# A decoder block's cross-attention: the output product of each head as two fp32r products instead of one fp32 product

## What is computed

```python
q, k, v = (heads(q), heads(k), heads(v))            # 16 heads of 64; 2,113 keys
scale = 1.0 / np.sqrt(np.sqrt(DIM_HEAD))
logits = jnp.einsum('bhqd,bhkd->bhqk', q * scale, k * scale)
w = jax.nn.softmax(logits.astype(jnp.float32), axis=-1).astype(logits.dtype)
out = jnp.einsum('bhqk,bhkd->bhqd', w, v)
out = out.transpose(0, 2, 1, 3).reshape(b, l, INNER)
return out @ Wout                                   # 1,024 -> 256
...
x = _layernorm(x + _L0_xattn_ref(ctx_1024, x, ...), axis=-1)
```

## Time and profile before

| | |
|---|---|
| time, median of 3 runs | 3040.41 us (3039.42 to 3043.43) |
| the profiled execution | 3045.14 us, span of the core 3043.4 us |
| TensorE busy over the span | 2881.4 us, 95% |
| VectorE, ScalarE, GpSimd | 2025.4, 1638.5, 1560.1 us |
| mean granted TensorE clock | 0.981 of full speed |

### The profile page before, as it was taken

One profiled execution on the slowest core, in us unless ns is written; L12 is line 12 of the kernel. 1 busy time (PEld: TensorE's weight loads), 2 busy tenths in 40 slices (PEclk: granted clock), 3 DMA queues, 4 the chain that ended last, 5 costly groups with the idle time before them and its releaser, 6 DMA issues. The chain is left out here.

```text
span 3043.4 us, 36342 instructions
## 1 busy us (share of the span) xinstructions
PE 2881.4 (95%) x12032; PEld 1906.0 (63%) x12032; DVE 2025.4 (67%) x3451; ACT 1638.5 (54%) x2837; POOL 1560.1 (51%) x1235
## 2 busy tenths in 40 slices
PE   7577999999999999999999999999999999899997
PEld 3234565656665656565656565656777777687786
DVE  5897777775658677666687767566555555356666
ACT  5753545453545454535454545366777777525652
POOL 4495757670017575600175756003656667526764
PEclk9898999999999999999999999999999999799999
DMA  6453212111122121211221212110101100421112
GB/s 237 149 180 106 76 36 60 35 53 57 39 70 60 36 66 29 73 37 39 70 67 36 60 36 66 37 39 15 46 20 34 45 17 15 146 74 60 49 46 82
DMA packets 71694, 189.98 MB, mean 62 GB/s; under 512 B 8420, under 2 KB 39272, under 8 KB 63448
## 3 DMA queue, kind: packets, MB, share of 16 engines
q1 hardware_dynamic: 67096, 172.08, 18.7%
q0 software_dynamic: 3984, 15.60, 1.6%
q10 hardware_dynamic: 432, 0.01, 0.0%
HBM read 124.59 MB, written 28.44 MB: 50 GB/s over the span
## 5 line engine op out<-in xcount | busy, mean ns | idle before, releaser
L1148 ACT ACTIVATE a_carry<-a_st 128x512 f32<-128x512 f32 (+1 forms) x1088 | 649.4, 597 | 918.5 <-PE a_st L1590 905.5
L1610 PE MATMUL a_o<-a_carry,a_vals 128*65 128x512 f32 (+1 forms) x1632 | 835.6, 593 | 0.0
L1338 DVE TENSOR_REDUCE a_maxes<-a_mx 128x1 f32<-128x512 f32 x1016 | 677.5, 686 | 189.0 <-PE a_mx L1513 180.9
L964 POOL TENSOR_TENSOR a_plow<-a_carry,a_phigh 128x512 fp32r<-128x512 f32 (+1 forms) x272 | 349.0, 1290 | 259.8 <-ACT a_phigh L1151 256.2
L996 POOL TENSOR_TENSOR a_shared<-a_shared,a_bc 128x512 f32<-128x512 f32 x192 | 250.9, 1307 | 386.7 <-DVE a_shared L1268 386.7
L1590 PE MATMUL a_st<-a_q,a_kone 65*128 65x512 f32 (+1 forms) x1088 | 431.6, 397 | 0.0
L1268 DVE TENSOR_TENSOR_SCAN a_shared<-a_shared 128x512 f32<-128x512 f32 x192 | 290.3, 1514 | 15.9 <-POOL a_shared L983 14.6
L1589 PE MATMUL a_st<-a_q,a_keven 128*128 128x512 f32 (+1 forms) x544 | 295.9, 544 | 2.5 <-ACT a_carry L1148 1.6
L1589 PE MATMUL a_st<-a_q,a_kodd 128*128 128x512 f32 (+1 forms) x544 | 286.8, 527 | 0.0
L1513 PE MATMUL a_mx<-a_kodd,a_q 128*128 128x512 f32 x512 | 275.6, 554 | 10.3 <-DVE a_maxes L1338 9.0
L1590 PEld LDWEIGHTS a_st<-a_q,a_kone 65*128 65x128 f32 (+1 forms) x1088 | 202.0, 186 | 123.6 <-issue 93.2
(11 more groups left out here) (300 smaller groups left out, 5225.3 us busy)
## 6 DMA issues: line engine op xcount, KB each, us to landing
a_bc<-m_kept_bc SPq DMA_DIRECT2D x48, 512.0 KB, 3.7
a_wt<-a_w_split SPq DMA_DIRECT2D x15, 1536.0 KB, 8.6
a_kone<-a_keven SPq DMA_DIRECT2D x32, 528.5 KB, 4.5
a_kone<-a_kodd SPq DMA_DIRECT2D x32, 528.5 KB, 4.2
e_wall<-in_w_t_dram SPq DMA_DIRECT2D x27, 512.0 KB, 5.6
a_shared<-m_kept_bc SPq DMA_DIRECT2D x16, 512.0 KB, 3.9
a_w_split<-a_wt POOLq DMA_DIRECT2D x4, 1536.0 KB, 5.4
a_shared<-in_ctx_dram SPq DMA_DIRECT2D x4, 1536.0 KB
```

Source lines behind the costliest of these rows:

```text
L964: nc.gpsimd.tensor_tensor(p_low(s)[0:r], p_of(s % 4)[0:r], p_high(s)[0:r].bitcast(F32), ALU.subtract).then_inc(p_low_ready, 1)
L1148: nc.scalar.activation(p_of(s % 4)[0:r], st[0:r, s % 2], ACT.Exp, scale=SCALE).then_inc(exp_done, 1)
L1338: nc.vector.reduce_max(maxes[:, c, t:t + 1], mx_bank(g, i), AX_X).then_inc(mx_max, 1)
L1610: nc.tensor.matmul(ps_o[0:DH + 1, g % 2], vals[0:r, kt * HG + j, :], p_of(s % 4)[0:r], start=(kt == 0), stop=(kt == KT - 1)).then_inc(pv_d ...
```

## The change

The one fp32 product of 65 rows becomes two fp32r products into the same bank. The first multiplies high parts: the tile `a_oone` has the output's high part in rows 0 to 63, the sum's high part in row 64 and its low part in row 96 (SUM_LOW), with zeros between, so it takes 97 rows, and 258 columns, an even number. The second has 128 rows: `a_otwo` is the output's low part over its high part, `a_wotwo` the weights' high part over their low part. To make these, ScalarE copies `a_o` twice where it copied once, VectorE has a new piece "o" at tile 4 (`out_low`, two subtractions), and in every fourth head, at tile 12, a new piece "w" splits the loaded weights of four heads (`out_weights_high`, two copies on ScalarE, `out_weights_low`, one subtraction on VectorE). Weights are loaded into one raw buffer after the split of the group before; GpSimd clears other tiles before head 0.

```diff
     b, h = divmod(g, H)
+    if g > 0:
+        at[LAG + 1].append(("o", g - 1, 0))
+    if g % HG == 0:
+        at[12].append(("w", g // HG, 0))
...
             def load_wo(n):
-                sp.dma_start(wo_sb[0:DH, n % 2, :, 0:DM], wo_src[:, n % NG * HG:(n % NG + 1) * HG]).then_inc(wo_loaded, 16)
+                if n > 0:
+                    sp.wait_ge(wo_low, n)
+                sp.dma_start(wo_raw[0:DH], wo_src[:, n % NG * HG:(n % NG + 1) * HG]).then_inc(wo_loaded, 16)
...
-                nc.scalar.activation(o_sb[0:DH + 1, g % 2], ps_o[0:DH + 1, g % 2], ACT.Copy).then_inc(o_out, 1)
+                if g < 2:
+                    act.wait_ge(ones_set, 2)
+                nc.scalar.activation(o_one[0:DH + 1, g % 2], ps_o[0:DH + 1, g % 2], ACT.Copy)
+                nc.scalar.activation(o_two[DH:P, g % 2], ps_o[0:DH, g % 2], ACT.Copy).then_inc(o_out, 1)
+
+            def out_weights_high(n):
+                act.wait_ge(wo_loaded, 16 * (n + 1))
+                act.wait_ge(ones_set, 2)
+                if n > 0:
+                    act.wait_ge(ring_full, AT["O", HG * n - 1, TT - 1] + 1)
+                nc.scalar.activation(wo_one[0:DH, :, 0:DM], wo_raw[0:DH], ACT.Copy)
+                nc.scalar.activation(wo_two[0:DH], wo_raw[0:DH], ACT.Copy).then_inc(wo_high, 1)
...
+            def out_low(g):
+                dve.wait_ge(o_out, g + 1)
+                nc.vector.tensor_tensor(o_two[0:DH, g % 2], ps_o[0:DH, g % 2], o_one[0:DH, g % 2].bitcast(F32), ALU.subtract)
+                nc.vector.tensor_tensor(o_one[SUM_LOW:SUM_LOW + 1, g % 2], ps_o[DH:DH + 1, g % 2],
+                                        o_one[DH:DH + 1, g % 2].bitcast(F32), ALU.subtract).then_inc(o_low, 1)
+
+            def out_weights_low(n):
+                dve.wait_ge(wo_high, n + 1)
+                nc.vector.tensor_tensor(wo_two[DH:P], wo_raw[0:DH], wo_one[0:DH, :, 0:DM].bitcast(F32),
+                                        ALU.subtract).then_inc(wo_low, 1)
...
                     pe.wait_ge(o_out, g + 1)
+                    pe.wait_ge(o_low, g + 1)
                     if g % HG == 0:
-                        pe.wait_ge(wo_loaded, 16 * (g // HG + 1))
+                        pe.wait_ge(wo_low, g // HG + 1)
                 wait_bank(what)
-                nc.tensor.matmul(ring[:, bank(what), 0:DM + 1], o_sb[0:DH + 1, g % 2, t * P:(t + 1) * P],
-                                 wo_sb[0:DH + 1, g // HG % 2, g % HG], start=True, stop=True).then_inc(ring_full, 1)
+                nc.tensor.matmul(ring[:, bank(what), 0:DM + 2], o_one[0:SUM_LOW + 1, g % 2, t * P:(t + 1) * P],
+                                 wo_one[0:SUM_LOW + 1, g % HG], start=True, stop=False)
+                nc.tensor.matmul(ring[:, bank(what), 0:DM], o_two[:, g % 2, t * P:(t + 1) * P],
+                                 wo_two[:, g % HG], start=False, stop=True).then_inc(ring_full, 1)
```

More of the change, by code:

```diff
@@ L472 @@
 LAG = 3
+SUM_LOW = 96
 FD = 3
@@ L603 @@
 BEFORE, BEFORE_ACT, BEFORE_DVE = first("PE"), first("ACT"), first("DVE")
-AFTER = [("O", NH - 1, t) for t in range(TT)] + [("E", B - 1, 0), ("F", B - 1, 0)]
+AFTER = [("o", NH - 1, 0)] + [("O", NH - 1, t) for t in range(TT)] + [("E", B - 1, 0), ("F", B - 1, 0)]
 MADE = BEFORE + [x for g in range(NH) for kt in range(KT) for x in BESIDE[g][kt]] + AFTER
@@ L696, in attention @@
         vals = sb("a_vals", [P, KT * HG, DH + 1])
-        o_sb = sb("a_osb", [P, 2, S])
-        wo_sb = sb("a_wo", [P, 2, HG, DM + 1])
+        o_one = sb("a_oone", [P, 2, S], F32R)
+        o_two = sb("a_otwo", [P, 2, S], F32R)
+        wo_raw = sb("a_woraw", [P, HG, DM])
+        wo_one = sb("a_woone", [P, HG, DM + 2], F32R)
+        wo_two = sb("a_wotwo", [P, HG, DM], F32R)
         lat = shared[:, CTX_T * DM:CTX_T * DM + TT * DM].rearrange("p (t d) -> p t d", d=DM)
@@ L707, in attention @@
         w_out_first = early[:, (FX + FS) * S:(FX + FS + 2) * S].rearrange("p (c d) -> p c d", d=DM)
-        bc_first = [halves[:, 0], halves[:, 1], bc_early, o_sb[:]]
+        bc_first = [halves[:, 0], halves[:, 1], bc_early, o_two[:].bitcast(F32)]
         decay_first, dtu_bank = [mx[:, 0], mx[:, 1], ring[:, 1]], [ps_o[:, 0], ps_o[:, 1]]
@@ L740, in attention @@
         o_out = sem("a_o_out")
+        o_low = sem("a_o_low")
+        wo_high = sem("a_wo_high")
+        wo_low = sem("a_wo_low")
         mx_full = sem("a_mx_full")
@@ L906, in load_weights @@
                 sp.dma_start(wt[:].rearrange("p i k n -> p (i k n)").bitcast(F32), w_dram[n % NG]).then_inc(w_loaded, 16)
-                if n > 1:
-                    sp.wait_ge(ring_full, AT["O", HG * (n - 1) - 1, TT - 1] + 1)
                 load_wo(n)
@@ L943, in set_ones @@
                 s.then_inc(ones_set, 1)
-                nc.gpsimd.memset(wo_sb[DH:DH + 1], 0.0)
-                nc.gpsimd.memset(wo_sb[0:DH, :, :, DM:DM + 1], 0.0).then_inc(wo_cleared, 1)
+                one = wo_one[:].bitcast(F32)
+                nc.gpsimd.memset(o_one[DH:P].bitcast(F32), 0.0)
+                nc.gpsimd.memset(one[DH:P], 0.0)
+                nc.gpsimd.memset(one[0:DH, :, DM:DM + 2], 0.0).then_inc(wo_cleared, 1)
                 pool.wait_ge(wo_cleared, 1)
-                nc.gpsimd.memset(wo_sb[DH:DH + 1, :, :, DM:DM + 1], 1.0).then_inc(ones_set, 1)
+                nc.gpsimd.memset(one[DH:DH + 1, :, DM:DM + 1], 1.0)
+                nc.gpsimd.memset(one[SUM_LOW:SUM_LOW + 1, :, DM:DM + 1], 1.0).then_inc(ones_set, 1)
             def make_rstd(what):
@@ L1139, in make @@
                     decays(*what[1:])
+                elif what[0] == "w":
+                    out_weights_high(what[1])
             def exp(s):
@@ L1380, in make @@
                     row_max(what[1], what[2])
+                elif kind == "o":
+                    out_low(what[1])
+                elif kind == "w":
+                    out_weights_low(what[1])
                 elif kind == "O":
@@ L1597, in add_o @@
                     pe.wait_ge(o_out, g - 1)
+                    pe.wait_ge(o_low, g - 1)
                 if j == 0:
```

## The result

The change makes the kernel slower: 3147.74 us (median of 4 runs, 3144.38 to 3148.97) against 3041.92 us in runs of the kernel before on the same chip, a ratio of 1.035 with a 95% interval of 1.033 to 1.036. The forecast was 3076 us, 36 us more; it became 106. The sign held, the size did not, and the time lies outside the range.

A forecast was written before the change was run, and what follows sets the result against it. TensorE was taken to bound the kernel, waiting on VectorE's row maxima. Terms: -50 + 29 + 12 + 9 + 10 + 19 + 5 + 2 = +36 us, giving 3076 us; range 3012 to 3100, the forecast's own 3050 to 3100.

The forecast's parts named there:

- Products: TensorE's output products, tiles 6 to 9: each 0.43 us becomes 0.24, 256 of them save 50 us.
- the 5: Tiles 6 to 9: 0.4 us of the saving lost in 12 heads where VectorE lacks idle time, 5 us.
- No subtraction of one row is in the trace ... I take 0.69: VectorE's second subtraction in `out_low`, one row of 512: taken as 0.69 us, like 64 rows; 1.4 us together.
- The mechanism, results held up behind `out_low`: Tiles 3 to 5: `out_low`'s 1.4 us on VectorE delays the row maxima that TensorE waits for in tile 5.
- the four terms: Delays by head: odd 29 us, even 9 in batches 0 to 2; odd 12, even 10 in the last batch.
- Without a scan ahead of them it fits. 0.4 on average: Even heads, batches 0 to 2: maxima 0.7 us late in head 22, none without a scan; 9 us in all.
- ScalarE gets a second copy ... I take 0.5: ScalarE in tile 3: the second copy of a head's output, `o_two`, puts off what follows by 0.5 us.
- Weights: Every fourth head, tile 12: ten heads at 1.0 us, two with `norm_var` 1.4, four of last batch 1.5; 19 us.
- The rival on the faster side: Late maxima are made up within the head, so only part of the 86 us costs stays: 2990 to 3033; chance 0.2.
- Worse than forecast: Weights' split holds ScalarE back in last batch, or one-row subtractions wait for each other: 3100 or more; chance 0.08.
- outside the loop: At the end of attention, 0.5 + 1.4 us stand uncovered ahead of the last products: 2 us.

The follow-up runs named there:

- e14: The changed kernel without ScalarE's second copy of a head's output after the first two heads (old values used): 3105.69 us, ratio 1.021 to the kernel before.
- e13: The changed kernel's two products and all their preparation, each piece moved to where VectorE had idle time in the trace of before: 3014.41 us, ratio 0.9915.
- e3: The changed kernel with all fp32r products, but high and low parts made only for the first two heads and first weights, then reused: 3008.22 us, ratio 0.988.
- e6_three: The changed kernel with three fp32r products (65, 65, 64 rows) instead of two, one output copy and one subtraction, same places: 3146.09 us, ratio 1.033.

## Why the prediction was right or wrong

- **Products: the price right, what is kept of it not.** 0.12 us start to start each. The forecast was -50, with 5 not given back. Alone they gave 37 us, so 13 us were not given back: tiles 6 to 9 gain 0.68 us a head for 0.78, and 6.5 us come back in tiles 10 to 14. The row that the 5 rest on is one head's.
- **"No subtraction of one row is in the trace ... I take 0.69": right**, 690 ns. The Trainium skill, "VectorE: DVE Perf Modes", section on the TRN2 errata, gives 0.691 us for 512 elements, with no term for the rows; this trace agrees.
- **The mechanism, results held up behind `out_low`: right.** Tiles 4 and 5 lose 98 us where the four terms made 60. The wrong sizes, by the tile times: odd heads of batches 0 to 2, 39 for 29; even heads there, 27 for 9 (1.6 of it in head 0, which has no `out_low`); odd heads of the last batch 16 for 12, even ones 16 for 10.
- **The step that failed most: "Without a scan ahead of them it fits. 0.4 on average".** It didn't fit in any even head: 0.8 us is the least, 1.1 the mean in batches 0 to 2. The margin was in the trace of before and was read in one head alone, head 22, whose 0.7 us late were taken for the bad case. In every one of the 23 even heads of batches 0 to 2 the first maximum behind the insertion ended only 0.44 to 0.70 us ahead of the product that needs it (0.66 in most, head 22 among them), and 1.4 us were put in front of it: 1.4 less 0.66, with the 0.06 between a maximum's end and its product, is the 0.8 measured. In heads 10, 26 and 42, where a scan also stands behind `out_low`, it is 2.1 to 2.5 us.
- **"ScalarE gets a second copy ... I take 0.5": too small.** 0.48 was the step from the one copy to the decay. Now the second copy starts 0.60 after the first, and what follows starts 0.61 after it. It costs 0.73, and 42 us together with what hangs on it (e14). Why the second copy is left no earlier is not shown. It isn't that both read `a_o`: the step behind it is 0.61 whatever comes next, and the weights' two copies, which also share a source, are 0.95 apart at a length of 1.05. It is the only one of these copies that writes other rows (64 to 127) than it reads (0 to 63).
- **Weights: 19 forecast, 28.8 at tiles 15 and 16.** Head 24 came out as worked out, 1.8, and the ten ordinary heads lost 10.4 together for 10. The heads that also have `norm_var`, forecast 1.4, lost 4.2 and 3.7, and the first head of the last batch, which has it too, 5.6: in VectorE's queue the statistics stand behind the weights' subtraction and ahead of the maxima, so they are put off as well. Each of the three also has a stretch at half clock there.
- **The clock: a term that was missing.** After some waits of 1.0 to 3.2 us TensorE falls to 1.2 GHz for a while. This is at most 27 us of the 106, and some 18 by the heads compared above. The Trainium skill, "TensorE: Matmul & The Clock Gate", Part 1, says that TensorE slows down when it has idled, and its account of the oscillation warns of stalls that bring the slow clock back; the trace agrees in that, though the page doesn't tell which of these short waits does it. It was to be weighed in the forecast of a change that adds stalls.
- **The rival on the faster side: wrong for this placement**, since the maxima were not made up within a head. It is what e13 reaches by other placing. *Worse than forecast*, 0.08, is what happened, though by another mechanism than the one named there.

Together, by the tile sums: 98 for 60 at tiles 4 and 5 (38 us), 29 for 19 at the weights (10), -29 for -45 in all other tiles, the products' (16), 4 for 2 outside the loop (2), and 4 more between the profiled spans (101.8 apart) and the medians (105.8): 70 of 70 us. The last 4 have no cause here; they are what one execution differs from a median. The half-clock stretches are inside the other terms, most plainly in tiles 6 to 9, which gain 43.0 us without them (e3) and 33.7 with. Their 18 us are an estimate from five stretches; no two kernels differ in the stretches alone.

## What to carry to other kernels

Work that is "hidden" on an engine two thirds busy costs its full length if it stands in front of a result that an in-order queue is waiting for: find a place by the idle time per tile, and put it behind the urgent results of that tile, before asking whether the new arithmetic is cheaper. Before work is inserted, read the margin between the first result behind it and whoever waits for that result, in every kind of head and not in one; and read all results behind it, here the K tile's low part as well as the maxima. Stalls have a second price where the slow clock follows them.

## What the runs showed of the hardware

- **64 rows after 65.** A product of 64 rows among products of 65 to 128 costs 0.28 us more than one of 65 rows (0.64 us for three, then 0.36), 74 to 78 us over the kernel. Columns behave otherwise: in the last batch of e6_three value products of 65, 64 and 65 columns start at 2282.09, 2282.33 and 2282.56. The Trainium skill, "TensorEngine Tiling (Array Packing)", Key Properties, says that a change of tiling mode drains TensorE, and lists 64 rows as a mode of its own; the rows agree with it. It lists 64 columns beside 128 rows as a mode too, and there these rows show no such cost.
- **VectorE beside GpSimd.** The weights' subtraction, two operands in SBUF, takes 1.22 us at tile 12 of the change in 13 of 16 heads and 1.36 in three, and a median of 2.12 in e13_by_room, where in most heads GpSimd is already multiplying when it starts. In the three heads with 1.36 it starts 0.24 us ahead of GpSimd's multiplication, and that takes 2.27 us where most take 1.27: both are stretched, the later one more. The Trainium skill, "SBUF — State Buffer", Who interferes with whom, states that a VectorE instruction with two SBUF inputs contends with a GpSimd one that reads SBUF; the trace agrees. The subtractions out of `a_o`, with one SBUF operand, stay at 0.68 and 0.69.

```profile
L1397 DVE TENSOR_TENSOR a_wotwo<-a_woraw,a_woone x16: 1218/2115/2191, 329.3 to 2505.8; 64x1024 fp32r<-64x1024 f32 x16
```
